# Attention and recurrence on one core: scores of four heads in one run, transposed probabilities in the dense banks

## The reference

```
# layer 0: attention of 16 heads of 32, with one image key and value in front
qkv = x @ c_attn_w + c_attn_b ;  q, k, v = split(qkv)
k = concat([img @ uk_w.T + uk_b, k]) ;  v = concat([img @ uv_w.T + uv_b, v])
scores = q @ k.T / sqrt(32), causal, + mask ;  attn = softmax(scores)
x = x + (attn @ v) @ c_proj_w + c_proj_b
# layer 1: a recurrence over the 512 tokens, for 8 sequences at once
h[t] = tanh(h[t-1] @ Wh + x[t] @ Wx + b)          (h[-1] = cond)
out = x + h
```

## Time and profile before

| | |
|---|---|
| median of three runs | 1738.16 us (1734.18 to 1741.51) |
| the profiled execution | 1743.1 us, of which the span 1741.3 |
| PE (TensorE matmul) busy | 1654.6 us, 95% |
| PEld (weight loads) busy | 1263.7 us, 73% |
| DVE (VectorE) busy | 798.4 us, 46% |
| ACT (ScalarE) busy | 670.5 us, 39% |
| POOL (GpSimd) busy | 184.6 us, 11% |
| TensorE clock granted, mean | 0.976 |

### The profile page before, as it was taken

How to read it: one execution, slowest core, us unless ns; L and a number is a source line. 1 busy time by engine, 2 the same in 40 slices (tenths; PEclk the granted TensorE clock), 3 DMA queues, 4 the chain that set the end, 5 groups by cost and what they waited for, 6 DMA issues and landing times.

```text
span 1741.3 us, 74131 instructions
## 1 busy us (share of the span) xinstructions
PE 1654.6 (95%) x32749; PEld 1263.7 (73%) x32749; DVE 798.4 (46%) x2687; ACT 670.5 (39%) x2257; POOL 184.6 (11%) x300
## 2 busy tenths in 40 slices
PE   6889999999999999999999999999999999999775
PEld 6667777787777778777777777777677677767654
DVE  3444444444445454454545455454554454544221
ACT  3433333433334334443434443443443443434111
POOL 2111010111011101101011110111100101100000
PEclk8868999999999999999999999999999999999998
DMA  6222121221223222232323333233332343321000
GB/s 234 78 52 65 42 57 51 63 67 56 57 59 87 62 75 68 82 88 73 85 66 98 89 85 93 60 103 98 88 98 73 103 108 94 92 69 35 15 9 14
DMA packets 167903, 130.24 MB, mean 75 GB/s; under 512 B 54264, under 2 KB 153112, under 8 KB 167072
## 3 DMA queue, kind: packets, MB, share of 16 engines
q1 hardware_dynamic: 153792, 92.92, 19.1%
q0 software_dynamic: 13792, 32.58, 6.7%
HBM read 100.00 MB, written 25.43 MB: 72 GB/s over the span
## 4 chain that ended last, share of the span: by engine, by line
PE 89%; issue 3%; DVE 2%; DMA 2%; ACT 2%; SPq 1%; POOL 0%; DVEq 0%; ACTq 0%; POOLq 0%
PE rec L1044 26%; PE scores L963 11%; PE turned L974 11%; PE dense L492 8%; PE dense L493 7%; PE dense L494 7%; PE rec L1035 6%; PE pv L991 5%; PE pv L1009 2%; PE scores L1044 2%; DVE pre L870 1%; ACT states L724 1%; PE dense L945 1%; PE dense L1051 1%; SPq L517 1%
## 5 line engine op out<-in xcount | busy, mean ns | idle before, releaser
L1044 PE MATMUL rec<-wh,states 128*32 128x128 f32 x15360 | 516.4, 275 | 27.0 <-ACT states L724 25.8
L1044 PEld LDWEIGHTS rec<-wh,states 128*32 128x32 f32 x15360 | 399.7, 110 | 123.3 <-ACT states L724 64.3
L676 ACT ACTIVATE probs<-probs,nmax 128x64 f32<-128x64 f32 (+7 forms) x512 | 271.6, 531 | 269.7 <-DVE nmax L815 266.6
L870 DVE STREAM_TRANSPOSE pre<-rec 128x128 f32<-128x128 f32 x480 | 151.7, 316 | 471.4 <-PE rec L1044 470.6
L724 ACT ACTIVATE states<-pre 128x32 f32<-128x32 f32 x512 | 133.1, 260 | 455.3 <-DVE pre L870 453.3
L815 DVE CUSTOM_DVE_ANT_0 probs<-scores,msk,nimg 128x64 f32<-128x64 f32 (+7 forms) x512 | 249.9, 514 | 62.8 <-PE scores L963 54.4
L974 PE MATMUL turned<-ident,probs 128*128 128x128 f32 (+1 forms) x1280 | 242.9, 292 | 7.9 <-ACT probsT L683 7.2
L963 PE MATMUL scores<-kt,q 32*64 32x64 f32 (+7 forms) x2048 | 231.4, 431 | 0.3 <-DVE nmax L815 0.2
L974 PEld LDWEIGHTS turned<-ident,probs 128*128 128x128 f32 (+1 forms) x1280 | 132.5, 135 | 90.4 <-issue 66.3
L824 DVE COPY probsT<-turned 128x128 f32<-128x128 f32 (+3 forms) x256 | 124.8, 487 | 78.4 <-PE turned L974 72.8
L683 ACT COPY probsT<-turned 128x128 f32<-128x128 f32 (+3 forms) x256 | 106.8, 417 | 115.3 <-PE turned L974 114.8
(11 more groups left out here) (148 smaller groups left out, 1817.4 us busy)
## 6 DMA issues: line engine op xcount, KB each, us to landing
vbuf<-v_dram SPq DMA_DIRECT2D x64, 192.0 KB, 2.8
xin<-x SPq DMA_DIRECT2D x64, 128.0 KB, 2.9
v_dram<-vbuf POOLq DMA_DIRECT2D x64, 128.0 KB, 2.7
out<-outs POOLq DMA_DIRECT2D x32, 256.0 KB, 4.2
vbuf<-v_dram SPq DMA_DIRECT2D x64, 128.0 KB, 2.4
kt<-k_dram SPq DMA_DIRECT2D x16, 512.0 KB, 4.1
vbuf<-v_dram SPq DMA_DIRECT2D x32, 256.0 KB, 3.4
k_dram<-knew POOLq DMA_DIRECT2D x60, 128.0 KB, 2.6
```

The lines of the kernel that those rows point to most:

```text
L676: act.activation(probs[:, g % PROBS, 0:n], probs[:, g % PROBS, 0:n], ACT.Exp, scale=-1.0, bias=nmax[:, e, h:h + 1], accum_out=rowsum[:, e, ...
L870: dve.transpose(pre_all, rec_bank(g // GROUP)[:, 0:P]).then_inc(pre_ready, 1)
L1044: last = pe.matmul(rec_bank(g // GROUP)[Q * j:Q * j + Q, 0:P], state_tile(g - 1)[:, f, :], wh[:, f, P * j:P * j + P], start=False, stop=f ...
```

## The change

Four things are changed together.

1. The scores of the four heads of a group are one event after another on PE, at every fourth unit, and each head has a bank of its own: `scores0` to `scores3`. No recurrence step is laid between them.
2. The banks `turned0` and `turned1` are gone. A `turn` takes `dense0` or `dense1` by turns with all the dense jobs; its own semaphores go too, and `pv` and the next user of the bank wait for `dense_copied`. So that a half-done `v` doesn't hold a bank past a `turn`, `v` follows `vfirst` at once.
3. `TURN_LAG` is 2 instead of 4 and `PV_LAG` 8 instead of 10.
4. The estimated weight of a score is 0.06 + 0.06 per 128 keys instead of 0.07 + 0.107. In the first block the copy to `probsT` takes only the 64 rows that hold keys. The four setup transpositions use the four `scores` banks.

```diff
-TURN_LAG = 4
-PV_LAG = 10
+TURN_LAG = 2
+PV_LAG = 8
...
         if u < HEADS:
-            if u % 2 == 0:
+            if u % HC == 0:
 
-                emit([("score", v, 0, 0.07 + 0.107 * keys(g) / P) for v in (u, u + 1)])
+                emit([("score", v, 0, 0.06 + 0.06 * keys(g) / P) for v in range(u, u + HC)])
...
             emit([side.pop(0)])
+            if out[-1][0] == "vfirst":
+                share -= side[0][3]
+                emit([side.pop(0)])
...
                 done += main[at][3]
+                if main[at][0] == "score" and main[at][1] % HC < HC - 1:
+                    continue
                 while t < STEPS and (done >= whole * (t + 0.5) / STEPS or at + 1 == last):
...
-        if kind in DENSE_KINDS and kind != "v":
+        if kind in DENSE_KINDS + ("turn",) and kind != "v":
             count = 2 if ("xsteps", 0, 0) in JOB else 3
...
-        scores = [ctx.enter_context(nc.psum_tensor(f"scores{i}", [P, BANK], F32)) for i in range(2)]
-        turned = [ctx.enter_context(nc.psum_tensor(f"turned{i}", [P, BANK], F32)) for i in range(2)]
+        scores = [ctx.enter_context(nc.psum_tensor(f"scores{i}", [P, BANK], F32)) for i in range(HC)]
...
-                    act.copy(probsT[:, g % TURNED, 0:n], turned[1][:, 0:n]).then_inc(turned_copied[1], 1)
+                    act.copy(probsT[rows, g % TURNED, 0:n], bank(kind, g, 0)[rows, 0:n]).then_inc(copied(kind, g, 0), 1)
...
-                    if g > 1:
-                        pe.wait_ge(shifted_ready, g - 1)
+                    if g >= HC:
+                        pe.wait_ge(shifted_ready, g - HC + 1)
...
                 elif kind == "turn":
                     pe.wait_ge(probs_ready, g + 1)
-                    if g > 1:
-                        pe.wait_ge(turned_copied[g % 2], g // 2)
+                    wait_bank(pe, kind, g, 0)
...
                 elif kind == "pv":
-                    for parity in range(2):
-                        pe.wait_ge(turned_copied[parity], 2 * g + 2)
+                    for held, count in turns_copied(g).items():
+                        pe.wait_ge(dense_copied[held], count)
```

More of the change, by code:

```diff
@@ L459, in wait_copied, with turns_copied @@
             eng.wait_ge(dense_copied[n], before + 1)
+        def turns_copied(group):
+            return dict((JOB["turn", g, 0][0], JOB["turn", g, 0][1] + 1) for g in range(HC * group, HC * group + HC))
         def heads_tile(group):
@@ L649, in _ @@
                 high_qkv(i)
-            for f, d in enumerate(scores + turned):
+            for f, d in enumerate(scores):
                 act.wait_ge(setup_turned, C + 2 + f)
@@ L679, in _ @@
                     n = P * tiles_of(g // UNITS)
+                    rows = slice(0, min(P, keys(g // UNITS)))
                     act.wait_ge(turned_ready, g + 1)
@@ L775, in _ @@
                     dve.wait_ge(setup_product, 2)
-                    dve.tensor_tensor(vimg_all, turned[0][:, :], uvb, ALU.add).then_inc(image_ready, 1)
+                    dve.tensor_tensor(vimg_all, scores[0][:, :], uvb, ALU.add).then_inc(image_ready, 1)
                     dve.wait_ge(image_ready, 1)
@@ L814, in _ @@
                         wait_copied(dve, "imgscore", trip, h // HC)
-                    dve.tensor_tensor_reduce(out=probs[:, g % PROBS, 0:n], in0=scores[g % 2][:, 0:n],
+                    dve.tensor_tensor_reduce(out=probs[:, g % PROBS, 0:n], in0=scores[g % HC][:, 0:n],
                                              in1=msk[:, e, 0:n], scale=-SCALE, scalar=nimg[:, trip % 2, e, h:h + 1],
@@ L823, in _ @@
                         dve.wait_ge(pv_done, (g - TURNED) // HC + 1)
-                    dve.tensor_copy(probsT[:, g % TURNED, 0:n], turned[0][:, 0:n]).then_inc(turned_copied[0], 1)
+                    dve.tensor_copy(probsT[rows, g % TURNED, 0:n], bank(kind, g, 0)[rows, 0:n]).then_inc(copied(kind, g, 0), 1)
                 elif kind == "imgprob":
@@ L933, in _ @@
                     for f in range(C):
-                        last = pe.matmul(turned[0][:, :], rbc[:, f, :], wh[:, f, :], start=f == 0, stop=f == C - 1)
+                        last = pe.matmul(scores[0][:, :], rbc[:, f, :], wh[:, f, :], start=f == 0, stop=f == C - 1)
                     last.then_inc(setup_product, 1)
@@ L962, in _ @@
                         at = W * (2 * e + b)
-                        last = pe.matmul(scores[g % 2][W * b:W * b + W, 0:n], q[rows, trip % 2, c, at:at + W],
+                        last = pe.matmul(scores[g % HC][W * b:W * b + W, 0:n], q[rows, trip % 2, c, at:at + W],
                                          heads_tile(group)[rows, b, :], start=True, stop=True, skip_group_check=True)
@@ L968, in _ @@
                     pe.wait_ge(probs_ready, g + 1)
-                    if g == 0:
-                        pe.wait_ge(image_ready, 1)
-                    if g > 1:
-                        pe.wait_ge(turned_copied[g % 2], g // 2)
+                    wait_bank(pe, kind, g, 0)
                     for at in range(0, n, P):
-                        last = pe.transpose(turned[g % 2][0:min(P, n - at), at:at + P],
+                        last = pe.transpose(bank(kind, g, 0)[0:min(P, n - at), at:at + P],
                                             probs[:, g % PROBS, at:min(at + P, n)], ident[:])
```

3 lines of the change are left out of this document (2 added, 1 removed).

## The result

The changed kernel takes **1821.07 us**, the median of four runs (1815.96 to 1823.36), beside 1739.84 (1734.18 to 1742.93) for the kernel before on the same chip: a ratio of 1.0467 [1.043, 1.0503]. It is 81 us slower; 65 us faster was forecast, and the range ended at 1722.

What follows compares the result with a forecast made beforehand. PE was taken as the bound until about 1600 us, then the recurrence's loop. 131 us of PE work removed less 66 us of waits gives 65 us less, 1738.2 to 1673 us; likeliest band 1647 to 1702, full range 1628 to 1722.

Steps and rivals of the forecast that it cites:

- Scores on PE: Score runs on PE: 313 runs costing 210 us become 128 costing 83 + 4 us, so 123 us less.
- the slow rival: Four heads don't run side by side on PE, a run costing two pairs: 1756 us, slower than before; chance 0.05.
- Exponentials in a row: A step's tanh stands on ACT behind four exponentials, so PE waits: 40 us in sum, 18 of it at 512 keys.
- The worked example: At 512 keys, a step and one turn after a run of four: PE stands 2.5 us waiting for tanh.
- Shared banks: Turns and dense jobs share two banks: 92 of 893 uses come before the copy is done, 26 us of waits.
- 26 + 15: Dense-bank waits: 26 us with the copying engine free, plus 15 for copies behind four shifts or four exponentials.
- the waits named as a sign: In the profile after, PE idle before turns and dense products, ended by copies at L834, L692 and proj sums: some 25 us.
- That transposed probabilities are asked for two units earlier costs nothing in the wide blocks: Shorter turn lag: with some 3 us a unit, a turn comes 6 us after its scores, exponential done at 2.7; cost nothing.
- they don't add ... I take three quarters.: PE's waits of 40 + 26 + 15 + 8 = 89 us overlap; three quarters, 66 us, taken, ends 40 and 95.
- the closer steps: Recurrence steps less than 1.81 us after the last: 46 intervals instead of 22, 8 us more waiting.
- PE's busy time was taken to fall by all the work removed: PE's work falls by 131 us, 123 from scores and 8 from turns, to a busy time near 1525 to 1540.
- Worse queues: ACT's and DVE's copies behind bursts hold both dense banks: waits of 95 to 125 us, 1702 to 1732 us; chance 0.18.

Runs made afterwards that it cites:

- short exponentials: Changed kernel with the exponential over the first 64 columns alone, other columns left out: 1786.7 us; the same edit in the kernel before: 1739.12 us.
- The repairs: Changed kernel with tanh ahead of the burst's second half (1803.86 us), x casts two units later (1813.25), norm and imgturn one unit sooner (1781.63); all three: 1771.07.
- the late x and the normalization: Kernel before with lags 2 and 8, norm and imgturn one unit sooner: 1799.89 us; then also x casts and their products two units later: 1775.92 us.
- the seven that were run: Changed kernel 1821.07 us; with tanh earlier 1803.86, casts later 1813.25, norm sooner 1781.63, these three 1771.07, last turn ahead of scores 1833.02, all four 1763.71.
- pairs left whole: Kernel before with no recurrence step laid between the two heads of a pair, 313 runs of scores becoming 256: 1702.42 us, ratio 0.9784.

## Why the prediction was wrong

- **Scores on PE: right.** 128 runs, 83 us and 128 x 0.03 expected; at 320 and 512 keys each costs what was forecast: four heads take 1.04 at 512 keys against 1.02 for the pair of the earlier trace rows. So the slow rival is out. The Trainium skill ("TensorE: Matmul & The Clock Gate", Part 3) states 3.07 times for four row tiles, from which the forecast made 1.30 of one head's time; this trace does not agree, with 0.73 for four heads against 0.69 for one at 320 keys.
- **Exponentials in a row: right in kind; in size only in the wide blocks.** The worked example is right to 0.2 us. From 384 keys on the wait for tanh grew by 25 us where 33 were forecast, in the narrower blocks by 26 where 7 were, so that 52 in all lies near the 40 partly by luck. Most of the narrow blocks' share is not the exponentials' length: between 160 and 990 us the wait for tanh is 33 us in the changed kernel, 16 with the casts of x later and 28 with short exponentials. And the forecast priced tanh alone, while everything on ACT's list behind the four waits: the bias copy costs PE 19.8 us against 5.0 with banks, lags and pairs, the copy before `rowturn` 14.0 against 2.2.
- **Shared banks: half again as large.** Without bursts the forecast has 26 us; banks alone cost 39 us of idle time and 44 of time, in part at `q` for `nimg`, the image score's minimum, and at `rowturn`, which were not named. That 44 is near 26 + 15 = 41 is luck. In the changed kernel the waits named as a sign (ended by the copies at L834 and L692 and by proj sums) come to 29 us, where some 25 were named. The sentence of the Trainium skill ("TensorEngine Tiling (Array Packing)", Performance Considerations) that copies out of PSUM may become the bottleneck was set aside by throughput; by throughput that stands, DVE being 43% busy, yet waits for copies are a good part of the loss.
- **The failed step: "That transposed probabilities are asked for two units earlier costs nothing in the wide blocks".** It costs 62 us alone. The working took the exponential as starting when its shift is done (done at 2.7 us after the scores, needed at 6) and looked at ACT's and DVE's lists as if they held scores alone. In the same lists stand the casts of x, which wait for a DMA issued only when the last projection's sum is done, and the normalization. The four units of lag were the cover for these; and the narrow blocks, where a unit is shorter and the waits are as long, were not priced at all.
- **Second: "they don't add ... I take three quarters."** In time banks and lags add: 44 + 62 = 106, and 106 measured (by the ratios 2.7 + 3.8 = 6.5% against 6.2%), where three quarters would be 80. The idle times of the profiled executions add less well, 39 + 54 against 78. The run of four brought 111 - 28 = 83 us of its own on top (PE's idle time from 165 to 245), where the forecast has 40 + 15 + 8 for the bursts and the closer steps. PE's idle time grew by 159 us where 66 was forecast. Why one wait does not give the others time here is not shown. My reading is that it would only where two waits meet at one place, while each engine's list is strict and the three hang on one another in a ring (PE to DVE to ACT to PE). The repairs, on the other hand, do overlap (50 us of 65).
- **Third: PE's busy time was taken to fall by all the work removed.** PE's busy time was forecast as 1525 to 1540 and is 1573.6, 34 to 49 us above. In the parts with unchanged work on PE, busy time went up with idle: banks +14 for +39, lags +18 for +54, both +30 for +78. More broken runs of scores are not the cause: these lists have 312, 304 and 303 runs, not more than the 313 of before. The lower clock explains a part of it, as in the 4 us at 0.50 shown above: 1 less the mean clock, times the span, is 42 us before and 75 after, so up to 33 us (part of this time PE was idle anyway). For the banks alone the mean clock is 0.981, no lower than before, and the +14 has another cause, which stays open.
- **"Worse queues"** was the right rival in kind. Its 95 to 125 us of waits were the end of the range; 159 came.

What stays open: how the loss divides between the two lags, why 38 us remain with the lags when the late x and the normalization are taken away, and whether any order with four heads in a run beats the kernel before. None of the seven that were run does; the best is 1.3% slower.

## What to carry to other kernels

Work taken off the full engine is worth its time only if the distances between producers and consumers stay: pairs left whole gave 39 us for 40 of busy time, with lags and banks as they were; on top of the shorter lags and shared banks the run of four gave no time at all beyond whole pairs. Before a lag is shortened, list everything in the queues between the two ends, above all instructions that wait for a DMA, and price the distance in every stretch, the narrow ones first. When a change has parts, time each part alone: the loss of 62 us from two constants would have been found in one run.

## What the runs showed of the hardware that was not expected

- A row strip of the array beside three others is nearly free at 128, 320 and 512 keys: four fp32 heads of 32 rows take 0.40 us at 128 keys (a run of before 0.38), 0.73 at 320 and 1.04 at 512 (the pair of before 1.02), one head 0.69 at 320, so 3.8 heads' worth of work in the time of one (4 x 0.69 / 0.73).
- PE's recorded busy time for the same instructions is no constant: 1654.6, 1668.8, 1673.0 and 1685.0 us for before, banks, lags and both, all with x32749 and with no more runs of scores, while idle was 87, 125, 141 and 165. Two kernels' busy times are compared only at like idle times.
- A wait of 3.38 us at one place was followed by 4 us at a granted clock of 0.50, the 1.2 GHz level, with PE busy throughout, before the clock came back (0.96 in the next 4 us). In the whole stretch from 320 to 520 us the clock fell from 1.00 to 0.97, with PE busy 178.6 of 200 us instead of 196.8.
